# A delta-rule recurrence on one core: the small triangular solve is started one slot earlier, the scores' transposes are put ahead of k's projection

## The chip, the cores and the metric

The kernel runs on one core of one Trainium2 chip. The metric is the time of one execution on the device in microseconds (us), as the median over several executions. TensorE is called PE in the profile, VectorE DVE, ScalarE ACT, GpSimd POOL, and SyncE, which issues all DMAs of this kernel, SP.

## The reference, cut to what matters

The input is x of shape (32, 512, 256). A gated delta-rule recurrence with 8 heads of 32 runs over the 512 tokens of each batch, two steps for each token; around it stand projections, a gate, a norm, an output projection, two layer norms and a feed-forward layer with merged low-rank weights.

```python
q, k, v = silu(x @ Wq), silu(x @ Wk), silu(x @ Wv)
log_f = log_sigmoid(x @ Wf1 @ Wf2);  beta = sigmoid(x @ Wbeta) * 2
k = l2norm(k);  k_ = -beta * k
gk = interleave(log_f, 0);  a = interleave(k_ * exp(log_f), k_);  bb = interleave(k, k)
kk, vv, qq = interleave(0, k), interleave(0, v), interleave(0, q)
for t:   # 1024 steps
    bS = einsum('bhk,bhkv->bhv', bb_t, S)
    S = exp(gk_t) * S + a_t * bS + kk_t * vv_t
    o_t = einsum('bhk,bhkv->bhv', qq_t, S)
y = rmsnorm(o[1::2] * sigmoid(x @ Wog1 @ Wog2)) * norm_w
x = layernorm(x + y @ Wo)
x = layernorm(x + x @ (W.T + lora.T) + b)
```

## The kernel before

The tokens are cut into 32 groups of 512 (2 x 16 batches, 16 tokens of each). The recurrence is run in blocks of 8 tokens (16 steps): inside a block the steps' dependence on each other is a 16 x 16 unit triangular matrix, whose inverse is worked out once, so that a block costs a few small matmuls. A group has 8 chunks of such blocks, and the program is a pipeline of iterations j, one for each group, each of 8 **slots** 0 to 7. In slot n of iteration j:

- PE runs `deltas` (L732) of the chunk before, `updates` (L724), `right_sides` (L741) of chunk n, and then `dense<n>`, the part of the dense work that is hung on this slot: v's projection and the first scores in slot 0, the gate and further scores in slot 1, `dense2` and `dense3` (k's and q's projections `project` L582, the scores' transposes `turn_scores` L614, the transposes `turn_rows` L624, the beta and f matmuls L596 and L599), the feed-forward (L634) in slot 4, the sums of squares (L605) in slot 5, the output projection (L695) in slot 6, the inverse's transposes (L706) in slot 7.
- DVE runs `update` (o_col L1105, change L1113; it waits for `updates` of this slot) and `turn_right_sides` (L1121, x_now L1124; it waits for `right_sides`), and then its own share of dense work. x_now is what `deltas` of the next slot need.
- ACT runs `delta_part` (L860, which waits for DVE's `update` of the slot), `query_part` (qs L881, which waits for x_now), `mask_part` (wa_now L874), and then its share.
- POOL adds and decays the state (L475, L479) after DVE's `update`, and adds the bias to h_row (L491, four instructions) between slots 3 and 4, once eight steps of the solve are done.

The dense work belongs to neighbouring groups: iteration j makes k, q, f and beta of group j + 2, scores and the inverse of group j + 1, and the output of groups j - 1 to j - 3. Each engine runs its instructions in the order in which they are written; semaphores carry the waits.

The inverse of group j + 1 is made like this. `turn_scores` transposes the scores a_low into PSUM (stage "nt", 4 fills); ACT sets inv to the identity (L977) and copies the fills into `low` (L990, 8 copies); `solve` on DVE runs 15 steps p = 0 to 14 of a product (L1162) and a sum (L1166) each; ACT spreads inv into `both` (L1051); PE transposes that in slot 7. Before the change `solve` runs its steps 0 to 7 at the end of slot 3, 8 to 10 and, behind the clamp of dd (L1228), 11 to 14 at the end of slot 4, and ACT spreads inv at the end of slot 5.

PSUM banks: three banks are handed round in the order of a list, `FILLS`, and `claim` makes PE wait until the bank's fill three places back in the list has been drained by ACT or DVE. From k on the list reads before: k0, k1, nt0, nt1, q0, q1, ht0, ht1, beta0, f0, ff0, ff1, yss0, yss1. So the second transposes of `turn_rows`, ht1, wait until q0 has been drained, that is for ACT's Silu of q (L1001), and f0 waits until ht0 has been drained (L1005).

Of the kernel before, what the change touches and what calls it, by code (L numbers as in the profile page):

```python
# [8 lines left out]
ACT = mybir.ActivationFunctionType  # L9
# [6 lines left out]
HF = D // P  # L16
HPH = P // HD
GB = 2
# [4 lines left out]
ROWS = TB * STEPS  # L23
# [51 lines left out]
def delta_block(nc, x, xt, wq, wk, wv, wf1, wf2, wbeta, wog1, wog2, norm_w, wo, ffn_wt, ffn_b,  # L75
# [8 lines left out]
    TILES = CH * CT  # L84
# [18 lines left out]
              "q": (2, HF), "beta": (2, HF), "f": (2, HF), "yss": (-1, HF), "kss": (2, HF), "nt": (1, 4),  # L103
              "wo": (-1, TT // 2), "tt": (1, 4)}
    PER_BANK = {s: GB if s == "nt" else 1 for s in STAGES}
    FILLS = [(s, i) for some in ("v", "gate", "small", "k", "nt", "q", "ht", ("beta", "f"), "ff", "yss", "kss", "wo", "tt")
             for i in range(2) for s in ((some,) if isinstance(some, str) else some)
             if i < (1 if s in ("beta", "f") else STAGES[s][1])]
    RING = 3
# [6 lines left out]
    with ExitStack() as ctx:  # L116
# [24 lines left out]
        small = sb("small", [P, TOK])  # L141
# [3 lines left out]
        k_col = sb("k_col", [P, HF, TOK])  # L145
# [4 lines left out]
        w_col = sb("w_col", [P, TILES, HD])  # L150
        w_row = [sb(f"w_row{c}", [P, TILES, HD]) for c in range(2)]
        gate = [sb(f"gate{c}", [P, HF, TOK]) for c in range(2)]
# [3 lines left out]
        inv = sb("inv", [P, ROWS, HPH, ROWS])  # L156
        both = sb("both", [P, ROWS, HPH, GB, ROWS])
# [50 lines left out]
        def bank(stage, i):  # L208

            if i >= 2:  # L210
                return psum[3 + i - 2]
            if i == 1 and stage in ("beta", "f"):
                return psum[3 if stage == "beta" else 4]
            return psum[5 + AT[(stage, i)] % RING]
# [9 lines left out]
        filled = {s: signal(f"{s}_filled", n) for s, (_, n) in STAGES.items()}  # L224
# [16 lines left out]
        w_turned = signal("w_turned", 1)  # L241
# [4 lines left out]
        inv_set = signal("inv_set", 1)  # L246
# [39 lines left out]
        def there(g):  # L286

            return 0 <= g < G if isinstance(g, int) else True
# [236 lines left out]
        def _(pe):  # L525
# [82 lines left out]
            def turn_scores(j):  # L608
                pe.wait_ge(low_copied.handle, low_copied.at(j + 1, CH))
                for k in range(4):  # L610
                    ps = claim(j, "nt", k)
                    for i in range(4):
                        src = a_low[:, 4 * k + i, :, :].rearrange("p b m -> p (b m)")
                        mm = pe.transpose(ps[:, i * P:(i + 1) * P], src, ident)  # L614
                    mm.then_inc(filled["nt"].handle, 1)
# [40 lines left out]
                    mm.then_inc(filled["small"].handle, 1)  # L656

            def dense2(j):
                if there(j + 2):
                    for f in range(HF):  # L660
                        project(j, "k", 0, f)
                if there(j + 1):
                    turn_scores(j)

            def dense3(j):
                if there(j + 2):
# [186 lines left out]
        def _(act):  # L853
# [68 lines left out]
            def iteration(j, c):  # L922
# [53 lines left out]
                if next_one:  # L976
                    act.activation(inv[:, :, :, :], cf[:, C_EYE:C_EYE + ROWS * ROWS].rearrange(  # L977
                        "p (i j) -> p i j", i=ROWS).unsqueeze(2).to_broadcast([P, ROWS, HPH, ROWS]),
                                   ACT.Copy).then_inc(inv_set.handle, 1)
                if front:  # L980
                    for f in range(HF):
                        act.wait_ge(filled["k"].handle, filled["k"].at(j + 2, f + 1))
                        act.activation(k_col[:, f, :], bank("k", f)[:, :], ACT.Silu).then_inc(drained["k"].handle, 1)
                if next_one:
                    for k in range(4):
                        act.wait_ge(filled["nt"].handle, filled["nt"].at(j + 1, k + 1))
                        src = bank("nt", k)[:, :].rearrange("p (i h b j) -> p i h b j", i=4, h=HPH, b=GB)
                        for b in range(GB):
                            half = slice(b * TILES, (b + 1) * TILES)
                            act.activation(low[half, 4 * k:4 * k + 4, :, :], src[half, :, :, b, :], ACT.Copy,  # L990
                                           scale=-1.0).then_inc(drained["nt"].handle, 1)

                scan_part(3)
                query(3)
# [29 lines left out]
                if front:  # L1024
                    act.activation(ss_col[:, :, :], k_col[:, :, :], ACT.Square).then_inc(k_squared.handle, 1)
                    act.wait_ge(e_floored.handle, e_floored.at(j + 2, 1))
                    act.activation(dd[:, :, :, 1:SLOTS], dd[:, :, :, 1:SLOTS], ACT.Ln,
                                   bias=one).then_inc(f_logged.handle, 1)

                scan_part(5)  # L1030
                query(5)
# [8 lines left out]
                if front:  # L1040
# [3 lines left out]
                                       bias=eps_l2).then_inc(drained["kss"].handle, 1)  # L1044
                    act.wait_ge(drained["kss"].handle, drained["kss"].at(j + 2, HF))
                    act.activation(ss_col[:, :, :], ss_col[:, :, :], ACT.Exp, scale=-0.5).then_inc(r_ready.handle, 1)
                if next_one:
                    act.wait_ge(solve_step.handle, solve_step.at(j + 1, 2 * (ROWS - 1)))
                    for b in range(GB):
                        half = slice(b * TILES, (b + 1) * TILES)  # L1050
                        act.activation(both[half, :, :, b, :], inv[half, :, :, :], ACT.Copy).then_inc(inv_spread.handle, 1)  # L1051

                scan_part(6)
                query(6)
# [20 lines left out]
        def _(dve):  # L1075
# [50 lines left out]
            def mask_pair(g, c, k):  # L1126
                for i in reversed(range(PAIR)):
                    if i:
                        made = held(dve, until, a_filled.at(g, k + 1))
                        dve.wait_ge(set_up.handle, N_SET_UP)  # L1130
                        dve.wait_ge(a_filled.handle, made)
                    else:
                        made = held(dve, until, low_copied.at(g, PAIR * k + 1))
                        dve.wait_ge(set_up.handle, N_SET_UP)
                        dve.wait_ge(low_copied.handle, made)
                    src = a_banks[i][:, :, :, ROWS:RQ]
                    dve.copy_predicated(chunk(aq[c], PAIR * k + i).rearrange("p m (b t) -> p m b t", b=GB),  # L1137
                                        ci[:, :].rearrange("p (b t) -> p b t", b=GB).unsqueeze(1).to_broadcast(
                                            list(src.shape)), src).then_inc(aq_masked.handle, 1)
# [29 lines left out]
            def iteration(j, c):  # L1169
# [32 lines left out]
                turn_part(1)  # L1202
                if next_one:
                    mask_pair(j + 1, 1 - c, 2)
                    mask_pair(j + 1, 1 - c, 3)

                scan_part(2)
                turn_part(2)
                if next_one:
                    for i in range(2):  # L1210
                        some = slice(i * TILES // 2, (i + 1) * TILES // 2)
                        last = dve.transpose(w_row[1 - c][:, some, :], w_col[:, some, :])
                    last.then_inc(w_turned.handle, 1)

                scan_part(3)
                turn_part(3)
                if next_one:
                    dve.wait_ge(inv_set.handle, inv_set.at(j + 1, 1))
                    dve.wait_ge(drained["nt"].handle, drained["nt"].at(j + 1, 4 * GB))
                    solve(j + 1, 0, 8)  # L1220

                scan_part(4)
                turn_part(4)
                if next_one:
                    solve(j + 1, 8, 11)
                if front:
                    dve.wait_ge(drained["f"].handle, drained["f"].at(j + 2, HF))
                    dve.tensor_scalar(dd[:, :, :, 1:SLOTS], dd[:, :, :, 1:SLOTS], MAX_FALL, None,  # L1228
                                      ALU.min).then_inc(e_floored.handle, 1)
                if next_one:  # L1230
                    solve(j + 1, 11, ROWS - 1)

                scan_part(5)
                turn_part(5)
# [124 lines left out]
```

## Time and profile before

| | |
|---|---|
| median of 3 runs | 2539.0 us (2536.97 to 2541.99) |
| profiled execution, its own time | 2536.87 us |
| its span | 2535.0 us |
| PE busy | 2121.5 us (84%) |
| DVE busy | 1764.5 us (70%) |
| ACT busy | 1627.2 us (64%) |
| POOL busy | 838.3 us (33%) |
| the chain that ended last | PE 57%, DVE 22%, issue 15%, ACT 5%, DMA 1% |

The span is the profiled execution from its first to its last instruction; its own time has 1.87 us around that. The chain is followed back from the last instruction to what released each wait; that it passes through both PE and DVE says that in some slots PE's own work sets the pace and in others DVE's.

### The profile page before, as it was taken

The numbers are of one execution on the slowest core, as the hardware profiler recorded it, in microseconds if no ns is written. First come the engines' busy times: TensorE is split into PE (matmuls) and PEld (weight loads), VectorE is DVE, ScalarE is ACT, GpSimd is POOL, SyncE is SP. The second block draws the span as 40 slices with busy tenths as digits, with TensorE's granted clock in tenths as the row PEclk, the third lists the DMA queues.
The fourth block names the chain that finished last, engine by engine and source line by source line (L and its number), as shares of the span: only waits on it lengthen the run. The fifth ranks groups of instructions, "written<-read, shape, count | busy, mean of one in ns | idle before, by whom it ended". The sixth has DMA issues, their size and how long they took to land.

```text
span 2535.0 us, 191611 instructions
## 1 busy us (share of the span) xinstructions
PE 2121.5 (84%) x85960; PEld 1591.0 (63%) x85960; DVE 1764.5 (70%) x4196; ACT 1627.2 (64%) x3048; POOL 838.3 (33%) x805
## 2 busy tenths in 40 slices
PE   6777888888888888888888888888888888889784
PEld 3556666666666666666666666666666666666573
DVE  3567567777766777766777766677876677776643
ACT  3656566666666666666666666666667666666554
POOL 1133233333333333323333323333333333332330
PEclk8889999999999999999999999999999999999886
DMA  3343244443344444344444344444334444433431
GB/s 100 85 120 113 90 132 136 139 130 98 120 130 139 133 129 121 105 123 138 137 131 131 96 124 136 131 139 128 111 117 124 137 137 132 130 98 120 131 111 38
DMA packets 558366, 305.46 MB, mean 120 GB/s; under 512 B 417186, under 2 KB 517152, under 8 KB 558240
## 3 DMA queue, kind: packets, MB, share of 16 engines
q1 hardware_dynamic: 558240, 304.19, 40.4%
q14 instruction: 97, 0.79, 0.1%
q8 instruction: 29, 0.48, 0.1%
HBM read 35.66 MB, written 16.78 MB: 21 GB/s over the span
## 4 chain that ended last, share of the span: by engine, by line
PE 57%; DVE 22%; issue 15%; ACT 5%; DMA 1%; SPq 0%; DVEq 0%; ACTq 0%
PE bank L582 15%; PE bank L716 8%; PE bank L741 7%; PE wide L724 7%; PE wide L732 4%; DVE uq_a L1162 4%; DVE inv L1166 4%; ACT t_t L890 3%; DVE dd L1248 3%; PE bank L655 3%; PE bank L614 2%; DVE change L1113 2%; PE bank L605 2%; PE bank L599 2%; DVE k_col L1267 2%
## 5 line engine op out<-in xcount | busy, mean ns | idle before, releaser
L475 POOL TENSOR_TENSOR state<-state,change 128x512 f32<-128x512 f32 x252 | 347.2, 1378 | 1354.2 <-DVE change L1113 1354.2
L582 PE MATMUL bank<-x_col,w_kqv 128*128 128x512 f32 x768 | 372.4, 622 | 55.9 <-issue 43.7
L741 PE MATMUL bank<-uq_now,s_now 32*32 32x24 f32 x32768 | 364.4, 187 | 9.0 <-issue 7.3
L741 PEld LDWEIGHTS bank<-uq_now,s_now 32*32 32x32 f32 x32768 | 350.4, 105 | 14.4 <-issue 10.2
L724 PE MATMUL wide<-wa_now,delta 32*32 32x80 f32 x16512 | 350.2, 234 | 3.2 <-ACT wa_now L874 2.5
L860 ACT ACTIVATE delta<-wide 128x256 f32<-128x256 f32 x256 | 98.1, 383 | 388.0 <-DVE change L1113 383.6
L1137 DVE COPY_PREDICATED aq<-ci,bank 128x128 f32<-128x128 int32 x256 | 77.3, 302 | 346.7 <-PE bank L716 218.3
L724 PEld LDWEIGHTS wide<-wa_now,delta 32*32 32x32 f32 x16512 | 308.3, 108 | 4.9 <-DMA wa_now<-aq 2.8
L479 POOL TENSOR_TENSOR state<-state,edge 128x512 f32<-128x512 f32 x252 | 292.7, 1161 | 19.8
L732 PEld LDWEIGHTS wide<-x_now,t_now 32*32 32x32 f32 x16448 | 174.0, 108 | 149.0 <-issue 148.6
L1105 DVE TENSOR_TENSOR o_col<-qs,wide 128x64 f32<-128x64 f32 x512 | 89.2, 215 | 252.2 <-PE wide L724 249.9
L582 PEld LDWEIGHTS bank<-x_col,w_kqv 128*128 128x128 f32 x768 | 139.5, 195 | 197.7 <-issue 181.6
L732 PE MATMUL wide<-x_now,t_now 32*32 32x32 f32 x16448 | 200.7, 197 | 59.0 <-issue 41.5
L874 ACT ACTIVATE wa_now<-w_row,cf 128x256 f32<-128x256 f32 x512 | 229.6, 498 | 0.8
L1166 DVE TENSOR_TENSOR inv<-inv,uq_a 128x60 f32<-128x60 f32 (+7 forms) x480 | 217.0, 452 | 16.5
L1162 DVE TENSOR_TENSOR uq_a<-low,inv 128x60 f32<-128x60 f32 (+7 forms) x480 | 200.5, 418 | 17.4 <-ACT low L990 4.1
L1113 DVE STREAM_TRANSPOSE change<-wide 128x256 f32<-128x256 f32 x512 | 197.9, 424 | 1.3
L881 ACT ACTIVATE qs<-bank 128x128 f32<-128x128 f32 x256 | 70.9, 277 | 177.1 <-DVE x_now L1124 177.0
L918 ACT ACTIVATE a_low<-bank 128x256 f32<-128x256 f32 x256 | 134.0, 625 | 72.1 <-PE bank L716 71.9
L716 PEld LDWEIGHTS bank<-uq_a,w_a 32*32 32x32 f32 x8192 | 99.8, 109 | 111.1 <-issue 111.1
L491 POOL TENSOR_TENSOR h_row<-h_row,bias_row 128x256 f32<-128x256 f32 x128 | 89.0, 726 | 225.1 <-DVE inv L1166 172.9
L716 PE MATMUL bank<-uq_a,w_a 32*32 32x48 f32 x8192 | 108.7, 208 | 59.0 <-issue 58.9
(96 smaller groups left out, 3827.4 us busy)
## 6 DMA issues: line engine op xcount, KB each, us to landing
s_now<-state SPq DMA_DIRECT2D x256, 256.0 KB
uq_now<-uqv SPq DMA_DIRECT2D x256, 192.0 KB
t_now<-t_t SPq DMA_DIRECT2D x256, 128.0 KB
uq_a<-uqv SPq DMA_DIRECT2D x64, 384.0 KB, 3.1
low<-uqv SPq DMA_DIRECT2D x64, 384.0 KB
x_col<-in_xt_dram SPq DMA_DIRECT2D x32, 512.0 KB, 3.9
w_a<-w_col SPq DMA_DIRECT2D x64, 256.0 KB, 3.7
inv<-w_col SPq DMA_DIRECT2D x64, 256.0 KB
```

The lines of the kernel that those rows point to most:

```text
L475: pool.tensor_tensor(mine, mine, change[m % 2][:, :, :, :].rearrange("p m b v -> p (m b) v"), ALU.add).then_inc(s_added.handle, 1)
L479: pool.tensor_tensor(mine, mine, decay.unsqueeze(2).to_broadcast([P, CT * GB, HD]), ALU.mult).then_inc(state_ready.handle, 1)
L582: mm = pe.matmul(ps[:, :], w_kqv[:, a, w, f * P:(f + 1) * P], x_col[:, a, :], start=a == 0, stop=a == KT - 1)
L716: mm = pe.matmul(a_banks[m // CT][quarter(h), m % CT, :, :].rearrange("p b r -> p (b r)"), w_a[c][quarter(h), m, :], uq_of(uq_a[c], m % HF ...
L724: mm = pe.matmul(up_bank[quarter(h), m % HF, m // HF, :].rearrange("p (k e) -> p k e", e=PIECE), delta[quarter(h), m, :], wa_now[quarter(h ...
L732: mm = pe.matmul(p2_bank[quarter(h), m % HF, m // HF, :], t_now[quarter(h), m, :], x_now[quarter(h), m, :], start=True, stop=True)
L741: mm = pe.matmul(p1_bank[quarter(h), m, b, :], s_now[quarter(h), m, b, :], uq_of(uq_now, m % HF)[quarter(h), m // HF, b * RQ:(b + 1) * RQ] ...
L874: act.activation(dst, rows, ACT.Copy, scale=cf[:, C_TAKE + b:C_TAKE + b + 1]).then_inc(w_masked.handle, 1)
L918: act.activation(a_low[:, :, :, n * CT:(n + 1) * CT].rearrange("p i b m -> p m b i"), a_banks[i][:, :, :, 0:ROWS], ACT.Copy).then_inc(low_ ...
L1113: last = dve.transpose(dst[:, f, :, :], up_bank[:, f, :, 0:GB * HD])
L1162: dve.tensor_tensor(step, low[:, p + 1:ROWS, :, p:p + 1].to_broadcast(size), inv[:, p:p + 1, :, 0:width].to_broadcast(size), ALU.mult).the ...
L1166: dve.tensor_tensor(inv[:, p + 1:ROWS, :, 0:width], inv[:, p + 1:ROWS, :, 0:width], step, ALU.add).then_inc(solve_step.handle, 1)
```

## The change

- `FILLS`: nt now stands before k, so from there on the list reads nt0, nt1, k0, k1, q0, q1, ht0, ht1 and so on; ht1 stands three places behind q0 as before.
- PE: in slot 2 the scores' transposes run before k's projection.
- ACT: in slot 2 the 8 copies into `low` run before the two Silus of k; the two copies into `both` run at the end of slot 4 in place of slot 5.
- DVE: the two transposes of W (w_row) run in slot 1, between the third and the fourth pair of masks, in place of slot 2; `solve` runs steps 0 to 6 at the end of slot 2 and 7 to 14 at the end of slot 3; in slot 4 only the clamp of dd is left.

```diff
-    FILLS = [(s, i) for some in ("v", "gate", "small", "k", "nt", "q", "ht", ("beta", "f"), "ff", "yss", "kss", "wo", "tt")
+    FILLS = [(s, i) for some in ("v", "gate", "small", "nt", "k", "q", "ht", ("beta", "f"), "ff", "yss", "kss", "wo", "tt")
...
             def dense2(j):
-                if there(j + 2):
-                    for f in range(HF):
-                        project(j, "k", 0, f)
                 if there(j + 1):
                     turn_scores(j)
+                if there(j + 2):
+                    for f in range(HF):
+                        project(j, "k", 0, f)
...
+                if next_one:
+                    act.wait_ge(solve_step.handle, solve_step.at(j + 1, 2 * (ROWS - 1)))
+                    for b in range(GB):
+                        half = slice(b * TILES, (b + 1) * TILES)
+                        act.activation(both[half, :, :, b, :], inv[half, :, :, :], ACT.Copy).then_inc(inv_spread.handle, 1)
 
                 scan_part(5)
...
                 if next_one:
                     mask_pair(j + 1, 1 - c, 2)
-                    mask_pair(j + 1, 1 - c, 3)
-
-                scan_part(2)
-                turn_part(2)
-                if next_one:
                     for i in range(2):
                         some = slice(i * TILES // 2, (i + 1) * TILES // 2)
                         last = dve.transpose(w_row[1 - c][:, some, :], w_col[:, some, :])
                     last.then_inc(w_turned.handle, 1)
+                    mask_pair(j + 1, 1 - c, 3)
+
+                scan_part(2)
+                turn_part(2)
+                if next_one:
+                    dve.wait_ge(inv_set.handle, inv_set.at(j + 1, 1))
+                    dve.wait_ge(drained["nt"].handle, drained["nt"].at(j + 1, 4 * GB))
+                    solve(j + 1, 0, 7)
 
                 scan_part(3)
                 turn_part(3)
                 if next_one:
-                    dve.wait_ge(inv_set.handle, inv_set.at(j + 1, 1))
-                    dve.wait_ge(drained["nt"].handle, drained["nt"].at(j + 1, 4 * GB))
-                    solve(j + 1, 0, 8)
+                    solve(j + 1, 7, ROWS - 1)
 
                 scan_part(4)
                 turn_part(4)
-                if next_one:
-                    solve(j + 1, 8, 11)
                 if front:
                     dve.wait_ge(drained["f"].handle, drained["f"].at(j + 2, HF))
                     dve.tensor_scalar(dd[:, :, :, 1:SLOTS], dd[:, :, :, 1:SLOTS], MAX_FALL, None,
                                       ALU.min).then_inc(e_floored.handle, 1)
-                if next_one:
-                    solve(j + 1, 11, ROWS - 1)
```

The rows on PE in the loop over the groups, slots 2 and 3, with the number of each PSUM bank and the semaphores that are waited for (L582 in slot 2 is k's projection and in slot 3 q's; rows with L620 belong to ht1, those with L599 to f). Before the change:

```order
L582 MATMUL bank5<-x_col,w_kqv 128x512 [waits gate_drained]
L582 MATMUL bank3<-x_col,w_kqv 128x512 [waits gate_drained]
L614 MATMUL bank4<-cf,a_low 128x128 [waits small_drained]
L614 MATMUL bank5<-cf,a_low 128x128 [waits k_drained]
L582 MATMUL bank3<-x_col,w_kqv 128x512 [waits k_drained]
L620 REGISTER_ALU [waits q_drained]
L624 MATMUL bank3<-cf,h_row 128x128 [waits h0_normed]
```

And after it:

```order
L614 MATMUL bank5<-cf,a_low 128x128 [waits gate_drained]
L614 MATMUL bank3<-cf,a_low 128x128 [waits gate_drained]
L582 MATMUL bank4<-x_col,w_kqv 128x512 [waits small_drained]
L582 MATMUL bank5<-x_col,w_kqv 128x512 [waits nt_drained]
L582 MATMUL bank3<-x_col,w_kqv 128x512 [waits nt_drained]
L620 REGISTER_ALU [waits q_drained]
L624 MATMUL bank3<-cf,h_row 128x128 [waits h0_normed]
L599 MATMUL bank5<-small,w_second 128x512 [waits ht_drained]
```

The transposes L614 have moved ahead of the first two L582 (k); the second k now waits for the first drain of nt, and the waits of slot 3 on q_drained and ht_drained are where they were.

The rows on DVE around the end of the solve's part in slot 2. In the changed program step 6 of the solve ends ahead of slot 3's `update` (L1105, L1113), and step 7 stands behind its x_now:

```order
L1166 TENSOR_TENSOR inv<-inv,uq_a 128x36x7
L1105 TENSOR_TENSOR o_col<-qs1,wide 128x4x2x8 x2
L1113 STREAM_TRANSPOSE change1<-wide 128x4x64 x2
L1121 TENSOR_TENSOR bank0<-bank0,uqv1 128x16x8
L1124 STREAM_TRANSPOSE x_now<-bank0 128x256
L1162 TENSOR_TENSOR uq_a<-low,inv 128x256
```

In the program before, the same five rows of slot 3 stood behind the transposes of W:

```order
L1212 STREAM_TRANSPOSE w_row0<-w_col 128x1024 x2
L1105 TENSOR_TENSOR o_col<-qs1,wide 128x4x2x8 x2
L1113 STREAM_TRANSPOSE change1<-wide 128x4x64 x2
L1121 TENSOR_TENSOR bank0<-bank0,uqv1 128x16x8
L1124 STREAM_TRANSPOSE x_now<-bank0 128x256
L1162 TENSOR_TENSOR uq_a<-low,inv 128x60
```

What was step 0 behind slot 3's x_now is now step 7, and seven steps have moved from behind `update` to ahead of it.

## Rows read from the trace of the kernel before

**Rows 1.** Timeline of PE: start, length (us), line, tiles, count [idle before <-releaser].

```profile
1209.77 0.75 PE L732 MATMUL wide<-x_now,t_now 32*32 32x32 f32 x64
...
1222.81 1.53 PE L706 MATMUL bank<-cf,both 128*128 128x128 f32 x12 [0.73 <-DVE x_row L1287]
...
1231.89 1.56 PE L716 MATMUL bank<-uq_a,w_a 32*32 32x48 f32 x128 [1.80 <-issue]
...
1252.13 3.70 PE L582 MATMUL bank<-x_col,w_kqv 128*128 128x512 f32 x8 [0.55 <-issue]
...
1257.50 0.75 PE L732 MATMUL wide<-x_now,t_now 32*32 32x32 f32 x64
...
1264.88 1.04 PE L624 MATMUL bank<-cf,h_row 128*128 128x128 f32 x8
...
1266.21 0.69 PE L599 MATMUL bank<-small,w_second 32*128 32x512 f32 x1
...
1268.12 0.75 PE L732 MATMUL wide<-x_now,t_now 32*32 32x32 f32 x64
...
1275.60 0.75 PE L732 MATMUL wide<-x_now,t_now 32*32 32x32 f32 x64
...
1281.57 1.13 PE L605 MATMUL bank<-r_col,cf 128*128 128x512 f32 x2 [0.98 <-DVE h_row L1239]
...
1284.34 0.75 PE L732 MATMUL wide<-x_now,t_now 32*32 32x32 f32 x64
```

**Rows 2.** Timeline of DVE, slots 1 to 5 of the same iteration.

```profile
1247.89 0.30 DVE L1137 COPY_PREDICATED aq<-ci,bank 128x128 f32<-128x128 int32 x1 [2.64 <-PE bank L716]
...
1252.34 2.33 DVE L1212 STREAM_TRANSPOSE w_row<-w_col 128x1024 f32<-128x1024 f32 x2
1259.48 0.35 DVE L1105 TENSOR_TENSOR o_col<-qs,wide 128x64 f32<-128x64 f32 x2 [4.81 <-PE wide L724]
...
1263.15 0.27 DVE L1162 TENSOR_TENSOR uq_a<-low,inv 128x112 f32<-128x112 f32 x1
...
1267.91 0.43 DVE L1162 TENSOR_TENSOR uq_a<-low,inv 128x256 f32<-128x256 f32 x1
...
1271.35 0.30 DVE L1121 TENSOR_TENSOR bank<-bank,uqv 128x128 f32<-128x128 f32 x1 [0.21 <-PE bank L741]
...
1272.06 1.20 DVE L1162 TENSOR_TENSOR uq_a<-low,inv 128x252 f32<-128x252 f32 x1
...
1278.80 0.22 DVE L1162 TENSOR_TENSOR uq_a<-low,inv 128x60 f32<-128x60 f32 x1
...
1279.22 0.35 DVE L1105 TENSOR_TENSOR o_col<-qs,wide 128x64 f32<-128x64 f32 x2
...
1280.86 1.25 DVE L1239 TENSOR_TENSOR h_row<-h_row,bank 128x512 f32<-128x512 f32 x2
```

**Rows 3.** Timeline of ACT, slots 2, 3 and 5 of the same iteration.

```profile
1253.42 1.07 ACT L977 ACTIVATE inv<-cf 128x1024 f32<-128x1024 f32 x1
...
1256.36 3.18 ACT L990 ACTIVATE low<-bank 64x256 f32<-64x256 f32 x8
...
1262.51 1.04 ACT L997 ACTIVATE r_col<-y_col 128x1024 f32<-128x1024 f32 x1
1263.45 0.58 ACT L1001 ACTIVATE q_col<-bank 128x512 f32<-128x512 f32 x1
...
1265.57 1.08 ACT L1005 ACTIVATE a_low<-bank 128x512 f32<-128x512 f32 x2
...
1281.94 1.48 ACT L1035 ACTIVATE r_col<-bank,cf 128x512 f32<-128x512 f32 x2
```

**Rows 4.** Timeline of POOL around the end of slot 3.

```profile
1268.97 2.78 POOL L491 TENSOR_TENSOR h_row<-h_row,bias_row 128x256 f32<-128x256 f32 x4 [5.98 <-DVE inv L1166]
1271.70 1.28 POOL L475 TENSOR_TENSOR state<-state,change 128x512 f32<-128x512 f32 x1
```

**Rows 5.** Windows, end of another iteration's slot 5: engines' busy time, granted clock, DMA.

```profile
1133.00:1136.60 3.60, 3.60 (x9) 1.05 (x9) 3.57 (x5) 2.55 (x4) 0.27 (x1) 0.58 0.00 0
```

More of the change, by code:

```diff
@@ L658, in dense2 @@
             def dense2(j):
+                if there(j + 1):
+                    turn_scores(j)
                 if there(j + 2):
@@ L661, in dense2 @@
                         project(j, "k", 0, f)
-                if there(j + 1):
-                    turn_scores(j)
             def dense3(j):
@@ L979, in iteration @@
                                    ACT.Copy).then_inc(inv_set.handle, 1)
-                if front:
-                    for f in range(HF):
-                        act.wait_ge(filled["k"].handle, filled["k"].at(j + 2, f + 1))
-                        act.activation(k_col[:, f, :], bank("k", f)[:, :], ACT.Silu).then_inc(drained["k"].handle, 1)
                 if next_one:
@@ L991, in iteration @@
                                            scale=-1.0).then_inc(drained["nt"].handle, 1)
+                if front:
+                    for f in range(HF):
+                        act.wait_ge(filled["k"].handle, filled["k"].at(j + 2, f + 1))
+                        act.activation(k_col[:, f, :], bank("k", f)[:, :], ACT.Silu).then_inc(drained["k"].handle, 1)
                 scan_part(3)
@@ L1046, in iteration @@
                     act.activation(ss_col[:, :, :], ss_col[:, :, :], ACT.Exp, scale=-0.5).then_inc(r_ready.handle, 1)
-                if next_one:
[L1048 to L1051, printed above, removed]
                 scan_part(6)
@@ L1204, in iteration @@
                     mask_pair(j + 1, 1 - c, 2)
+                    for i in range(2):
+                        some = slice(i * TILES // 2, (i + 1) * TILES // 2)
+                        last = dve.transpose(w_row[1 - c][:, some, :], w_col[:, some, :])
+                    last.then_inc(w_turned.handle, 1)
                     mask_pair(j + 1, 1 - c, 3)
@@ L1209, in iteration @@
                 if next_one:
[L1210 to L1213, printed above, removed]
+                    dve.wait_ge(inv_set.handle, inv_set.at(j + 1, 1))
+                    dve.wait_ge(drained["nt"].handle, drained["nt"].at(j + 1, 4 * GB))
+                    solve(j + 1, 0, 7)
                 scan_part(3)
```

## The prediction

> **What bounds the kernel now.** The table of the front matter gives the chain as PE and DVE in turns, so I did not read the shares of the whole span but one iteration of the loop, engine by engine. The first view is the timeline of PE. An iteration runs from `deltas` at 1209.77 to the same instruction at 1284.34, 74.57 us [rows 1]. Slot 3 begins at 1257.50, slot 4 at 1268.12, slot 5 at 1275.60 and slot 6 at 1284.34 [rows 1]. The reader should look at the idle time before each row. In slots 2 to 4 there is none but some 0.6 us of branching ahead of the dense part, so there PE's own work sets the pace. In slot 5 the second sum of squares waits 0.98 us for DVE's h_row; in slot 7 the transposes wait 0.73 us for DVE's x_row; in slot 0 the scores stand idle for 1.80 us [rows 1], because their operands are staged by a DMA that waits for the last DVE product of group j + 2. So from slot 5 to slot 0 DVE sets the pace.
>
> The second view is the timeline of DVE. It shows why. In slot 2 DVE is idle for 4.81 us and in slot 1 for 2.64 us, but in slot 4 it works off the rest of the solve until the moment at which slot 5's `update` starts, 1279.22, and that start has no idle time before it [rows 2]. From there to the end of slot 7 DVE runs without a gap. Its train starts with h_row at 1280.86 [rows 2]; the iteration is as long as PE takes from the release in slot 0 to h_row, plus that train. What counts for the change is therefore one number: how much earlier or later h_row starts.
>
> **What there is to gain.** With no solve in slot 4, h_row would start when PE lets it. In slot 4 L1121, released by PE's `right_sides`, started 1271.35 - 1268.12 = 3.23 us after the slot, and the next work 0.71 us behind it [rows 1, 2]. For slot 5 that is 1275.60 + 3.23 + 0.71 = 1279.54, against 1280.86 now: 1.32 us earlier. The 0.98 us of PE in slot 5 goes too. So the change can give some 1.0 to 1.3 us an iteration, and only if slot 5 begins no later than it does now.
>
> **What is free.** The transposes of W take 2.33 us and now stand in front of a mask that had 2.64 us of idle time before it [rows 2]; they fit, and if they did not, at most the difference would fall on scores that PE fills late in slot 1. The swap on PE costs nothing: the same instructions run, and the new wait of the second k for the drain of nt0 falls due after transposes and first k, by when ACT is through with it (below). The copies into `both` move from behind slot 5's work to a stretch of slot 4 in which ACT waited for DVE; they must be done by slot 7.
>
> **What it costs: slot 3's update is late.** This is the term that decides.
>
> (1) The transposes start at 1252.13, where k's projection did [rows 1]. ACT is not ready: it sets inv from 1253.42 for 1.07 us, and copies into `low` for 3.18 us [rows 3]. The copies end at about 1254.4 + 3.18 = 1257.6; before that `solve` can't start. DVE has been idle since x_now, about 1252.4.
>
> (2) Steps 1 to 6 took 1267.91 - 1263.15 = 4.76 us. Step 0 is as small as step 14, which took 1279.22 - 1278.80 = 0.42 us, plus the pipeline overlap, say 0.5 [rows 2]. No POOL work falls here. DVE is free at 1257.6 + 5.26 = 1262.85. Slot 3's `update` was released by PE at 1259.48 [rows 2]; it is late by 3.4 us. DVE alone could bear that: x_now would be made at some 1264.5, and PE's next `deltas` stand at 1268.12.
>
> (3) But ACT waits behind it. `delta_part` of slot 3 waits for `update`, and ACT is in order, so everything ACT does in slot 3 is queued behind it. In slot 5, where ACT followed `update` without other waits, its first dense work came 1281.94 - 1279.22 = 2.72 us after it [rows 2, 3]. The Square then takes 0.94 us up to the Silu of q0, and this 0.58 us [rows 3]. So q0 is drained at 1262.85 + 2.72 + 0.94 + 0.58 = 1267.1.
>
> (4) PE waits for that. ht0 is done at 1264.88 + 0.52 = 1265.4 [rows 1], and ht1 needs q0's bank. It runs from 1267.1 to 1267.65 and not to 1265.92: +1.7 us. f0 needs the drain of ht0. ACT comes to it after the second Silu, at about 1267.65, and one of the two copies takes 0.54 us [rows 3]; f0 starts at 1268.2 and not at 1266.21 [rows 1]: +2.0 us. Slot 4 begins at 1270.1 and slot 5 at 1277.6, 2.0 us later than now.
>
> (5) h_row then starts at 1277.6 + 3.23 + 0.71 = 1281.54, against 1280.86: +0.68 us. PE itself is 2.0 - 0.98 = 1.0 us late at slot 6, which is less than it waits for DVE in slots 6 to 0. So the iteration takes 0.68 us more.
>
> **The second half of the solve.** Steps 7 to 14 now run in slot 3 beside POOL's state work and, since step 7 comes at once, beside the four bias adds. An L1162 that takes 0.42 us alone took 1.20 us from 1272.06, while POOL's L475 ran from 1271.70 to 1272.98 [rows 2, 4]: each waited for the other's end. Undisturbed, the eight steps take about 6 us, the state work adds 1 us, and the bias adds something between nothing and their own 2.78 us [rows 4]; I take 2. They end at 1264.5 + 9 = 1273.5, or 1271.7 to 1274.5 by the bounds. Slot 4's `update` is released at 1270.1 + 1.98 = 1272.1 (1.98 is 1259.48 - 1257.50 [rows 1, 2]), so it is up to 2.4 us late; x_now follows 1.7 us behind, by 1276.2 at the latest, ahead of slot 5 at 1277.6. I cost it at nothing; its cover is thin, 1.4 us at the far bound. The Trainium skill, in "SBUF — State Buffer", section on who interferes with whom, has it that a DVE instruction with two SBUF inputs and a GpSimd instruction exclude each other for their whole length; by that rule the far bound, 2.78 us, holds rather than my 2, and the cover is the thin one. No bias add stands beside a solve in this trace.
>
> **The sum.** 28 of the 32 iterations have all parts (the first two have no turn_rows, the last two no q and no k). 28 x 0.68 = 19 us. On the profiled execution's own 2536.87 that is 2556; the median of the runs is 2.1 us above it, which makes 2558. I add 2 us for the clock (below) and forecast 2560 us, +0.8%. Differences under 0.2%, 5 us, are taken as none.
>
> **Rivals.**
>
> *The stall stays small and the gain comes (faster).* For: the solve leaves slot 4, where it is plainly in the way, and gain and loss differ by one small sum. Against: the loss is a chain of five measured lengths. The point that decides is how late slot 5 starts: 1.32 us or less instead of 2.0. That needs the low copies or the first seven steps to be 0.7 us shorter than in (1) and (2), or q0's drain to come early. With no stall at all the iteration is 1.0 to 1.3 us shorter: 2539 - 28 x 1.15 = 2507; with half of it about 2530. Chance 0.22.
>
> *Loss and gain cancel (no change).* Slot 5 is 1.2 to 1.5 us late. 2534 to 2544. Chance 0.08.
>
> *The clock falls in slot 3 (slower by more).* At the end of a slot 5 in which PE had stood idle twice, the granted clock was 0.58 for 3.60 us [rows 5], between the two levels of 1.2 and 2.4 GHz; at full clock the same work would take 3.6 x 0.58 = 2.1 us, so the fall cost 1.5 us. Not every iteration shows it. The new stall of 1.7 us lies between transposes and small matmuls in the stretch that is critical, so there a fall is paid in full, up to 28 x 1.5 = 42 us more; while slot 5 loses one of its idle times, which is worth nothing, since DVE is late there anyway. The Trainium skill, "TensorE: Matmul & The Clock Gate", section on why this matters, says that idle between bursts of matmuls takes the clock back to its half rate; by that rule each iteration might pay, the sum would be 2600, and it has a chance of its own in what follows. The slot 3 of before shows no fall. Chance 0.22 that a third or more of the iterations pay: 2570 to 2600.
>
> *The forecast as it stands*, only the stall and few falls: 2545 to 2570. Chance 0.48.
>
> **Numbers.** Slower by over 0.2%: 0.48 + 0.22 = 0.70. Same 0.08. Faster 0.22. The range leaves out the better half of the faster case (0.12) and the last of the clock's (0.05): 2524 to 2594. The likeliest case's own range is 2545 to 2570.
>
> **What would show it.** In the profile after: the copies into `low` end near 5.3 us after k's old start and DVE stands idle up to them, about 5 us in slot 2 (1); slot 3's `update` starts with no idle time, 3.4 us behind PE's release (2); ACT waits some 5 us for DVE's change in slot 3 (3); the transposes L624 are split, the second half with 1.7 us of idle time released by ACT's q_col, and slot 3 takes 12.6 in place of 10.62 us (4); slot 5 shrinks from 8.74 to 7.8 us (5). The forecast is wrong if L624 isn't split, if the granted clock is low in slots 3 and 4, or if x_now of slot 4 comes after PE's `deltas` of slot 5.

## The result, and the profile after

The changed kernel is slower: 2622.47 us in the median of 4 runs (2618.89 to 2629.29) against 2538.34, a ratio of 1.0332, 95% interval 1.0306 to 1.0359. The direction was forecast; the size was not: 84 us where 22 were expected, and 2622 lies outside the range of 2524 to 2594.

From the page of the changed kernel, the span, the engines' busy time and the engines' shares of the chain:

```profile
span 2617.6 us, 191583 instructions
PE 2175.2 (83%) x85960; PEld 1634.7 (62%) x85960; DVE 1772.5 (68%) x4196; ACT 1621.4 (62%) x3048; POOL 869.7 (33%) x805
...
PE 46%; DVE 26%; issue 15%; ACT 13%; DMA 0%; DVEq 0%; SPq 0%; ACTq 0%
```

PE is busy for 54 us more than before with the same number of instructions, and ACT, which had 5% of the chain, has 13%. Where that happens is seen in the timeline of PE, slots 2 to 5 of one iteration (the stretch that [rows 1] shows for before):

```profile
1212.47 1.96 PE L614 MATMUL bank<-cf,a_low 128*128 128x128 f32 x16 [0.65 <-issue]
...
1217.80 0.75 PE L732 MATMUL wide<-x_now,t_now 32*32 32x32 f32 x64
...
1225.16 0.60 PE L624 MATMUL bank<-cf,h_row 128*128 128x128 f32 x4
1227.47 0.65 PE L624 MATMUL bank<-cf,h_row 128*128 128x128 f32 x4 [1.70 <-ACT q_col L1001]
...
1230.69 1.06 PE L599 MATMUL bank<-small,w_second 32*128 32x512 f32 x1
1231.68 1.08 PE L732 MATMUL wide<-x_now,t_now 32*32 32x32 f32 x64
1232.55 2.34 PE L724 MATMUL wide<-wa_now,delta 32*32 32x80 f32 x64
...
1240.58 0.75 PE L732 MATMUL wide<-x_now,t_now 32*32 32x32 f32 x64
...
1244.43 1.98 PE L605 MATMUL bank<-r_col,cf 128*128 128x512 f32 x4 [0.68 <-issue]
```

The transposes L624 are split, and the second half waits 1.70 us for ACT's drain of q, as forecast. The wait of the second sum of squares in slot 5 is gone. What was not in the forecast's main case stands behind the stall: a matmul of f (L599) takes 1.06 us and `updates` (L724) 2.34 us. In the kernel before, at the same place, they took 0.59 and 1.31 us:

```profile
1267.61 0.59 PE L599 MATMUL bank<-small,w_second 32*128 32x512 f32 x1
...
1268.73 1.31 PE L724 MATMUL wide<-wa_now,delta 32*32 32x80 f32 x64
```

The windows of this stretch in the changed kernel, with PE's granted clock in the third column from the end, say why:

```profile
1223.00:1225.20 2.20, 2.20 (x7) 0.93 (x6) 2.17 (x8) 0.75 (x3) 0.99 (x1) 1.00 0.32 121
1225.20:1227.50 2.30, 0.60 (x6) 0.36 (x4) 2.20 (x4) 2.30 (x5) 1.77 (x3) 1.00 0.00 0
1227.50:1229.50 2.00, 2.00 (x9) 1.59 (x11) 1.93 (x3) 1.35 (x4) 2.00 (x3) 0.83 0.00 0
1229.50:1231.70 2.20, 2.20 (x9) 0.40 (x6) 2.06 (x5) 1.09 (x2) 1.05 (x2) 0.50 0.00 0
1231.70:1234.70 3.00, 3.00 (x133) 3.00 (x136) 1.94 (x7) 2.42 (x4) 0.00 (x0) 0.50 0.13 44
```

In the second window PE is busy for 0.60 of 2.30 us; in the windows after it the granted clock falls to 0.50, that is from 2.4 to 1.2 GHz, and it stays there into slot 4. In the next iteration slot 4 ran at 0.58 in the mean and took 10.85 us (first two lines below). One of the 27 iterations has the stall, 1.66 us, and no fall (last two lines):

```profile
1295.49:1308.47 12.98, 10.65 (x281) 6.56 (x280) 12.25 (x27) 6.55 (x13) 5.80 (x6) 0.96 0.16 51
1308.47:1319.32 10.85, 10.35 (x273) 9.02 (x272) 5.10 (x16) 7.87 (x12) 2.76 (x2) 0.58 0.19 60
...
2235.57:2248.00 12.43, 10.09 (x281) 6.58 (x280) 11.73 (x27) 6.24 (x13) 5.53 (x6) 1.00 0.16 53
2248.00:2255.48 7.48, 6.83 (x274) 6.00 (x273) 6.12 (x17) 5.35 (x10) 2.92 (x3) 1.00 0.27 88
```

That iteration took 74.75 us in all, no more than the 74.94 of before. Slots 3 and 4 of the kernel before, for comparison:

```profile
1257.50:1268.12 10.62, 9.94 (x281) 6.48 (x280) 7.93 (x21) 7.23 (x17) 2.31 (x2) 1.00 0.19 62
1268.12:1275.60 7.48, 6.82 (x273) 5.99 (x272) 5.76 (x13) 5.11 (x9) 5.11 (x6) 1.00 0.27 88
```

The mean length of each slot, read off the timeline of PE from one `deltas` to the next over 27 iterations of each kernel, in us:

| | slot 3 | slot 4 | slot 5 | slot 6 | slot 7 | slot 0 | slot 1 | slot 2 | iteration | slot 4 over 8 us |
|---|---|---|---|---|---|---|---|---|---|---|
| before | 10.63 | 7.48 | 9.22 | 7.58 | 6.98 | 13.17 | 10.75 | 9.13 | 74.94 | 0 of 27 |
| changed | 13.39 | 9.22 | 7.48 | 7.59 | 6.77 | 13.55 | 10.73 | 9.23 | 77.94 | 26 of 27 |

The iteration is 3.0 us longer; times 28 that is 84 us, the whole difference. Slots 3 and 4 lose 4.5 us, slot 5 gives back 1.7.

### The profile page after: what moved, and what is told of

Its sections match the earlier page's. It is cut to its first block, busy times and chain, and to the rows that moved or that the text cites. A ratio compares the mean times of both kernels' runs of the same rounds, so it can differ in the third digit from the quotient of the medians.

```text
span 2617.6 us, 191583 instructions
## 1 busy us (share of the span) xinstructions
PE 2175.2 (83%) x85960; PEld 1634.7 (62%) x85960; DVE 1772.5 (68%) x4196; ACT 1621.4 (62%) x3048; POOL 869.7 (33%) x805
## 4 chain that ended last, share of the span: by engine, by line
PE 46%; DVE 26%; issue 15%; ACT 13%; DMA 0%; DVEq 0%; SPq 0%; ACTq 0%
PE bank L716 8%; PE wide L724 7%; PE bank L741 7%; PE bank L582 6%; PE bank L634 5%; PE wide L732 4%; DVE dd L1245 3%; DVE uq_a L1162 3%; ACT t_t L890 3%; ACT low L986 3%; DVE inv L1166 3%; PE bank L655 3%; DVE change L1113 3%; DVE w_col L1275 2%; DVE x_now L1124 2%
## 5 line engine op out<-in xcount | busy, mean ns | idle before, releaser
L582 PE MATMUL bank<-x_col,w_kqv 128*128 128x512 f32 x768 | 371.2, 620 | 36.6 <-issue 24.1
L741 PE MATMUL bank<-uq_now,s_now 32*32 32x24 f32 x32768 | 372.5, 190 | 8.3 <-issue 8.3
L724 PE MATMUL wide<-wa_now,delta 32*32 32x80 f32 x16512 | 375.4, 244 | 3.6 <-ACT wa_now L874 2.5
L741 PEld LDWEIGHTS bank<-uq_now,s_now 32*32 32x32 f32 x32768 | 360.9, 108 | 12.7 <-issue 9.3
L724 PEld LDWEIGHTS wide<-wa_now,delta 32*32 32x32 f32 x16512 | 331.1, 114 | 6.5 <-DMA wa_now<-aq 2.8
L1162 DVE TENSOR_TENSOR uq_a<-low,inv 128x60 f32<-128x60 f32 (+7 forms) x480 | 210.5, 438 | 179.9 <-ACT low L986 165.6
L479 POOL TENSOR_TENSOR state<-state,edge 128x512 f32<-128x512 f32 x252 | 303.9, 1206 | 19.8
L732 PEld LDWEIGHTS wide<-x_now,t_now 32*32 32x32 f32 x16448 | 180.4, 110 | 191.1 <-issue 190.6
L732 PE MATMUL wide<-x_now,t_now 32*32 32x32 f32 x16448 | 207.2, 199 | 68.9 <-issue 40.7
L582 PEld LDWEIGHTS bank<-x_col,w_kqv 128*128 128x128 f32 x768 | 140.2, 196 | 177.7 <-issue 152.9
L1105 DVE TENSOR_TENSOR o_col<-qs,wide 128x64 f32<-128x64 f32 x512 | 88.9, 215 | 230.3 <-PE wide L724 226.2
L1113 DVE STREAM_TRANSPOSE change<-wide 128x256 f32<-128x256 f32 x512 | 197.8, 424 | 1.3
L634 PE MATMUL bank<-w_ffn,a_low 128*128 128x256 f32 x512 | 131.5, 414 | 19.4 <-issue 18.0
```

Source lines behind the costliest of these rows:

```text
L479: pool.tensor_tensor(mine, mine, decay.unsqueeze(2).to_broadcast([P, CT * GB, HD]), ALU.mult).then_inc(state_ready.handle, 1)
L582: mm = pe.matmul(ps[:, :], w_kqv[:, a, w, f * P:(f + 1) * P], x_col[:, a, :], start=a == 0, stop=a == KT - 1)
L634: mm = pe.matmul(ps[:, t * D:(t + 1) * D], h_col[:, a, own], w_ffn[:, a, :], start=a == 0, stop=a == KT - 1)
L724: mm = pe.matmul(up_bank[quarter(h), m % HF, m // HF, :].rearrange("p (k e) -> p k e", e=PIECE), delta[quarter(h), m, :], wa_now[quarter(h ...
L732: mm = pe.matmul(p2_bank[quarter(h), m % HF, m // HF, :], t_now[quarter(h), m, :], x_now[quarter(h), m, :], start=True, stop=True)
L741: mm = pe.matmul(p1_bank[quarter(h), m, b, :], s_now[quarter(h), m, b, :], uq_of(uq_now, m % HF)[quarter(h), m // HF, b * RQ:(b + 1) * RQ] ...
```

## The experiments

All were timed beside the kernel before on the same chip; ratios are to that kernel. The theory after the result: the stall is there as forecast and costs little, and the fall of the clock behind it costs the rest, in nearly every iteration.

**Only the orders.** The solve is put back to its old places, and the copies into `both` too. What is left is the order in slot 2, the list of banks and W's place.

```diff
-                    solve(j + 1, 0, 7)
...
-                    solve(j + 1, 7, ROWS - 1)
+                    solve(j + 1, 0, 8)
...
+                    solve(j + 1, 8, 11)
...
+                    solve(j + 1, 11, ROWS - 1)
```

> The changed kernel with the solve at its old places (steps 0 to 7 in slot 3, 8 to 14 in slot 4 around the clamp) and the copies into both back in slot 5; what stays of the change is the order in slot 2 (transposes before k, on PE and ACT, with the list of banks) and W's transposes in slot 1. Theory (stall and clock: the loss comes from the first seven steps of the solve ahead of slot 3's update): these orders are free, 2538 us, within 5. Rival (the new order in slot 2 or W's transposes cost something of their own): 2550 or more, with slot 1 or 2 longer than 10.7 and 9.2 us.

Measured: 2540.05 us, ratio 1.0013 (0.9999 to 1.0028), iteration 75.02 us. These parts are free; the loss comes with the solve's new places and the copies into `both`, which moved along with it.

**The stall filled.** The same changed kernel, with PE kept at work in it.

```diff
             def turn_rows(j):
                 for i in range(TT // 2):
+                    if i == 1 and there(j + 2):
+                        pe.wait_ge(drained["nt"].handle, drained["nt"].at(j + 1, 4 * GB))
+                        for a in range(KT):
+                            pe.matmul(psum[3][:, :], w_kqv[:, a, 1, 0:P], x_col[:, a, :],
+                                      start=a == 0, stop=a == KT - 1)
                     ps = claim(j, "ht", i)
```

> The changed kernel with two useless full matmuls (128x512, some 1.85 us together) on PE ahead of the wait for the drain of q0, into a bank that is free there and is overwritten later; nothing that is used is changed. PE has work where it stood idle for 1.7 us. Theory (of the loss in slots 3 and 4 about 2 us is the stall and the rest the fall of the granted clock that the idle time brings): the clock stays at full in slots 3 and 4, slot 3 takes 12.6 to 12.9 us, slot 4 again 7.5, and the time is what the prediction gave for the stall alone, 2555 to 2570. Rival (slot 4 is long because DVE comes late out of the solve that POOL's bias adds slow down, or for another reason on PE): slot 4 stays at 8.9 or more and the time at 2620.

Measured: 2548.28 us, ratio 1.0044 (1.0029 to 1.0060). The timeline of PE, where L622 is the filler, and the windows of slots 3 and 4 of that iteration:

```profile
1196.85 0.60 PE L629 MATMUL bank<-cf,h_row 128*128 128x128 f32 x4
1197.29 1.88 PE L622 MATMUL bank<-x_col,w_kqv 128*128 128x512 f32 x4
1199.15 0.65 PE L629 MATMUL bank<-cf,h_row 128*128 128x128 f32 x4
...
1201.96 0.75 PE L737 MATMUL wide<-x_now,t_now 32*32 32x32 f32 x64
```

```profile
1189.48:1201.96 12.48, 11.80 (x286) 7.22 (x285) 11.74 (x27) 6.27 (x14) 5.54 (x6) 1.00 0.17 53
1201.96:1209.44 7.48, 6.83 (x274) 5.99 (x273) 6.13 (x17) 5.34 (x10) 2.93 (x3) 1.00 0.27 88
```

ht1 starts as late as in the changed kernel, 2.3 us after ht0, and slot 3 takes 12.48 us. But the clock is 1.00 and slot 4 takes 7.48 us; it is 7.45 to 7.52 us in all 27 iterations. 74 of the 84 us are gone by adding 1.9 us of useless work to each iteration. So the fall of the clock is shown to be nearly the whole loss, and the rival, that slot 4 is long because DVE is late, is out. The one iteration of the changed kernel without a fall says the same with nothing added. The time is below the 2555 to 2570 of this expectation, and within the 2545 to 2570 that the forecast gave for the stall with few falls: an iteration takes 75.13 us, 0.19 over before and not 0.68.

**q drained early.** ACT's two Silus of q stand ahead of `delta_part` of slot 3.

```diff
+                if front:
+                    for f in range(HF):
+                        act.wait_ge(filled["q"].handle, filled["q"].at(j + 2, f + 1))
+                        act.activation(q_col[:, f, :], bank("q", f)[:, :], ACT.Silu).then_inc(drained["q"].handle, 1)
                 scan_part(3)
                 query(3)
```

> The changed kernel with ACT's two Silus of q put ahead of its share of slot 3's recurrence (delta_part), so that the drain of q0 no longer waits for DVE's late update. Theory (the stall comes through ACT's order): the idle time of 1.7 us before ht1 goes, the one of f0 for the drain of ht0 stays below 1 us, the granted clock stays near full, slot 3 takes 11.0 to 11.7 us, and with slot 5 shorter by 1.3 the time is 2505 to 2540. Rival (the late update of slot 3 costs by itself, through x_now, the state or POOL): slot 3 stays over 12 us and the time over 2580.

Measured: 2634.52 us, ratio 1.0379 (1.0356 to 1.0402). This missed. The timeline of PE and ACT in slot 3:

```profile
1232.60 1.04 PE L624 MATMUL bank<-cf,h_row 128*128 128x128 f32 x8
1233.57 1.12 PE L596 MATMUL bank<-small,w_second 8*128 8x512 f32 x2
1236.12 0.69 PE L599 MATMUL bank<-small,w_second 32*128 32x512 f32 x1 [1.43 <-ACT a_low L1005]
...
1238.69 1.08 PE L732 MATMUL wide<-x_now,t_now 32*32 32x32 f32 x64
```

```profile
1234.52 1.06 ACT L1001 ACTIVATE r_col<-y_col 128x1024 f32<-128x1024 f32 x1
1235.46 1.09 ACT L1005 ACTIVATE a_low<-bank 128x512 f32<-128x512 f32 x2
```

The stall only moved. ht0 and ht1 now run together, but f0 waits for the drain of ht0, which still stands behind ACT's recurrence and the Square, and that wait of 1.43 us brings the clock down as well: in this iteration the granted clock of slot 4 is 0.59, and slot 4 is over 8 us in 26 of 27. I had priced the wait at under 1 us, because I forgot the Square.

**All four drained early.** As the one before, with the drains of ht0 and ht1 moved along. The solve is cut as in the changed kernel.

```diff
+                if out_of:
+                    for i in range(TT // 2):
+                        act.wait_ge(filled["ht"].handle, filled["ht"].at(j - 2, i + 1))
+                        act.activation(h_col[:, :, 2 * i * P:2 * (i + 1) * P],
+                                       bank("ht", i)[:, :].rearrange("p (a t) -> p a t", a=KT),
+                                       ACT.Copy).then_inc(drained["ht"].handle, 1)
                 scan_part(3)
```

> The changed kernel with ACT's drains of q0, q1, ht0 and ht1 all ahead of its share of slot 3's recurrence; the solve stays cut 7 and 8, so DVE's update of slot 3 is as late as in the changed kernel. The run before this one moved only q's Silus, and the stall went from ht1 to f0. Theory (the late update costs only through ACT's order, and the rest is the clock): PE has no idle time in slot 3 but the branch, slot 3 takes 10.6 to 10.9 us, slot 4 7.5, the granted clock is full there, and the time falls to where the cut into 3, 7 and 5 steps is: 2495 to 2510. Rival (the late update costs by itself): slot 3 or 4 stay longer by 1 us or more, 2530 or more.

Measured: 2526.34 us, ratio 0.9971 (0.9957 to 0.9985). Slots 3 and 4 are as the theory has them, 10.63 and 7.53 us in the mean, at full clock:

```profile
1175.37:1185.98 10.61, 9.93 (x282) 6.47 (x281) 9.93 (x25) 4.76 (x12) 3.67 (x4) 1.00 0.19 63
1185.98:1193.55 7.57, 6.88 (x274) 6.01 (x274) 7.16 (x19) 4.85 (x9) 3.21 (x4) 1.00 0.27 87
```

DVE's update of slot 3 is as late as in the changed kernel, 5.30 us after the slot began, and it costs slot 3 nothing once ACT no longer carries it to PE. So the path of the stall is shown: DVE's solve, ACT's delta, ACT's drains, PE's banks. The time is 16 us above the expectation's upper end and under the rival's 2530. Most of that is in slot 0, 14.25 us in the mean, over 14.5 in 16 of 27 iterations; these iterations take 75.06 us, the other 11 take 73.45. In one of the long ones the clock in slot 0 was 0.89:

```profile
1140.77:1155.61 14.84, 11.90 (x520) 7.87 (x521) 10.18 (x32) 11.86 (x23) 5.73 (x8) 0.89 0.68 176
```

Why slot 0 is caught so much more often here than in the other kernels (before: 4 of 27) no run tells. Slot 5, 7.86 us here, is 0.38 longer than in the cut into 3, 7 and 5 steps below; that was not tried apart.

**The kernel before with a late ACT.** Nothing of the change; two more table loads on ACT.

```diff
+                act.preload_act_table_set("natural_log_exp_and_others")
+                act.preload_act_table(ACT.Silu)
                 if front:
                     for f in range(HF):
                         act.wait_ge(filled["q"].handle, filled["q"].at(j + 2, f + 1))
```

> The kernel before, with nothing of the change; ACT only loads its activation table twice more (1.28 us each by the profile) ahead of q's Silu in slot 3, so that q0 is drained some 2.6 us later. By the rows of before ht1 would wait about 1.2 us and f0 start 1.6 us later. Theory (idle time of PE at this place brings the clock down, whatever its cause): the granted clock falls in slots 3 and 4 of most iterations, slot 3 takes 12.2 us or more and slot 4 8.5 or more, 2590 to 2640. Rival (the fall needs what is particular to the changed kernel, the transposes ahead of k or the solve beside POOL): slot 3 takes 12.2, slot 4 7.5, about 2583.

Measured: 2622.92 us, ratio 1.0357 (1.0334 to 1.0379). The timeline of PE:

```profile
1219.58 0.65 PE L624 MATMUL bank<-cf,h_row 128*128 128x128 f32 x4 [1.41 <-ACT q_col L1003]
...
1222.67 1.06 PE L599 MATMUL bank<-small,w_second 32*128 32x512 f32 x1
1223.66 1.08 PE L732 MATMUL wide<-x_now,t_now 32*32 32x32 f32 x64
1224.54 2.34 PE L724 MATMUL wide<-wa_now,delta 32*32 32x80 f32 x64
```

A stall of 1.4 us of another cause brings the same fall: the granted clock is 0.50 from 1221.6 to 1226.7 here, and slot 4 is over 8 us in 17 of 27 iterations. In the others slots 3 and 4 take 12.18 and 7.48 us. So neither the transposes ahead of k nor the solve beside POOL is needed for it. That the time is the changed kernel's own is chance: the iterations without a fall take 76.13 us here, 1.2 more than before, because the solve still stands in slot 4 and slot 5 gives little back, and the falls bring the mean to 77.33. The length of the idle time does not alone decide how often it is caught: 1.41 us was caught in 17 of 27, but 1.43 us with q drained early in 26 of 27, as the 1.64 to 1.72 us of the changed kernel.

**Three, seven and five steps.** The stall is avoided where it begins: only as many steps stand ahead of slot 3's update as end by its release; the last five stand in slot 4 behind the clamp, and the copies into `both` in slot 5 again.

```diff
-                    solve(j + 1, 0, 7)
+                    solve(j + 1, 0, 3)
...
-                    solve(j + 1, 7, ROWS - 1)
+                    solve(j + 1, 3, 10)
...
+                    solve(j + 1, 10, ROWS - 1)
```

> The changed kernel with the solve cut otherwise: steps 0 to 2 in slot 2, 3 to 9 in slot 3, 10 to 14 in slot 4 behind the clamp; the copies into both back in slot 5. Three steps end about 1.9 us after the copies into low, when PE releases slot 3's update. Theory: no stall in slot 3 (10.6 us), slot 4 7.5, slot 5 7.5 to 7.8, and the gain of 1.0 to 1.3 us an iteration that the prediction named as what is to be had: 2500 to 2512. Rival (the end of the solve in slot 4 still holds DVE, or the train of DVE from h_row on is not what sets slots 5 to 0): 2530 to 2545.

Measured: 2497.75 us, ratio 0.9842 (0.9816 to 0.9868), faster than both kernels and 2 us under the range expected. The timeline of DVE at the start of slots 3 and 5, and the windows of slots 3, 4 and 5:

```profile
1159.21 0.26 DVE L1162 TENSOR_TENSOR uq_a<-low,inv 128x60 f32<-128x60 f32 x1 [5.20 <-ACT low L986]
...
1161.14 0.35 DVE L1105 TENSOR_TENSOR o_col<-qs,wide 128x64 f32<-128x64 f32 x2
...
1178.67 0.22 DVE L1166 TENSOR_TENSOR inv<-inv,uq_a 128x60 f32<-128x60 f32 x1
1179.21 0.35 DVE L1105 TENSOR_TENSOR o_col<-qs,wide 128x64 f32<-128x64 f32 x2 [0.31 <-PE wide L724]
...
1181.14 1.25 DVE L1238 TENSOR_TENSOR h_row<-h_row,bank 128x512 f32<-128x512 f32 x2
```

```profile
1159.17:1169.78 10.61, 9.93 (x281) 6.47 (x280) 9.71 (x24) 6.42 (x14) 3.50 (x4) 1.00 0.19 63
1169.78:1177.23 7.45, 6.81 (x273) 6.02 (x272) 6.74 (x14) 6.14 (x10) 4.90 (x5) 1.00 0.27 88
1177.23:1184.70 7.47, 6.77 (x265) 4.48 (x265) 6.77 (x18) 3.63 (x7) 2.32 (x2) 1.00 0.27 88
```

Slot 3's update starts 1161.14 - 1159.17 = 1.97 us after the slot, on time; slot 5's update now waits 0.31 us for PE, where before DVE was the late one, and slot 5 takes 7.47 us. An iteration takes 73.56 us, 1.38 less than before.

**Four, six and five steps.** The edit is shown against the version before this one.

```diff
-                    solve(j + 1, 0, 3)
+                    solve(j + 1, 0, 4)
-                    solve(j + 1, 3, 10)
+                    solve(j + 1, 4, 10)
```

> As the cut into 3, 7 and 5 steps, but 4, 6 and 5: slot 3's update is then 0.8 us late, and q0 is drained as much later, which the old order covered (it was drained 1.4 us before ht1 came to it). Both theories: no stall, within 5 us of the run with 3, 7 and 5, about 2498. If it is slower by 10 us or more, the cover is thinner than the rows said.

Measured: 2497.53 us, ratio 0.9853 (0.9833 to 0.9873), the same. The cover of q0's drain holds for a fourth step; between four steps and seven it is used up.

**A filler in slot 0.** In the version with 3, 7 and 5 steps.

```diff
             def dense0(j):
                 if there(j + 1):
                     project(j, "v", 2, 0)
+                if there(j) and there(j + 1):
+                    pe.wait_ge(drained["tt"].handle, drained["tt"].at(j, 4))
+                    for a in range(KT):
+                        pe.matmul(psum[3][:, :], w_kqv[:, a, 2, 0:P], x_col[:, a, :],
+                                  start=a == 0, stop=a == KT - 1)
```

> The cut into 3, 7 and 5 steps with two useless full matmuls on PE in slot 0, behind v's first projection, where PE stands idle 1.8 us before the first scores; their result is overwritten and used by nothing. In that kernel slot 0 takes 14.7 us in 8 of some 28 iterations with the clock low, and else 13.3 or 12.5. Theory (the same clock loss, in slot 0): no slot 0 over 13.6, 2483 to 2492. Rival (the two matmuls delay the scores, or slot 0 is long for the DMA's sake): 2497 or more.

Measured: 2499.82 us, ratio 0.9866 (0.9844 to 0.9889); against 0.9842 without the filler that is no gain. Both theories had a part: slot 0 is nowhere over 13.4 us (7 of 27 were over 14.5), but iterations whose slot 7 was long and whose slot 0 was then short, 12.3 to 12.7 us, now have 13.0 to 13.4 there. In the two traces the full iterations do get shorter, 73.35 us in place of 73.56, 6 us over 27 of them; but the first transposes of `turn_rows`, with which the start of the pipeline ends, stand at 301.15 us and not at 286.89. So in the iterations the filler takes back a part of what the clock gives, and the start takes the rest; what lengthened the start was not tried.

## Why the prediction was wrong

Right, and shown on the chip:

- (1) and (2): DVE is idle for 5.20 us up to the end of the copies into `low`, and its update starts 1223.09 - 1217.80 = 5.29 us after slot 3 began (the row of L1105 below) in place of 1.98, so 3.3 us late; 3.4 was forecast.
- (3) and (4): the stall sits where it was put, with 1.70 us, and at full clock it makes slot 3 12.46 us (the stall filled, where a filler of 1.88 us stands in its place) or 12.43 us (the one iteration without a fall) where 12.6 was forecast. That the late update reaches slot 3 only through ACT's order is shown by the version with all four drains early.
- The second half of the solve: 9 us were forecast. It runs from 1224.73 to the end of step 14, 1233.85, which is 9.1. POOL's four adds took 3.44 us beside it, and a product of 240 elements 0.81 where it takes 0.41 alone. Four of DVE's instructions were lengthened like this, by some 0.4 us each, 1.6 us in all, so the far bound of 2.78 us, which the prediction had by the Trainium skill, "SBUF — State Buffer", section on who interferes with whom, was not reached. Costing the second half at nothing was right: slot 4 is 7.49 us with the stall filled. (The bounds for its end come out of the prediction's own numbers as 1271.5 and 1274.3, not 1271.7 and 1274.5; nothing hangs on it.)

```profile
1222.76 0.42 DVE L1166 TENSOR_TENSOR inv<-inv,uq_a 128x252 f32<-128x252 f32 x1
1223.09 0.34 DVE L1105 TENSOR_TENSOR o_col<-qs,wide 128x64 f32<-128x64 f32 x2
...
1224.73 1.03 DVE L1162 TENSOR_TENSOR uq_a<-low,inv 128x256 f32<-128x256 f32 x1
...
1228.31 0.81 DVE L1162 TENSOR_TENSOR uq_a<-low,inv 128x240 f32<-128x240 f32 x1
...
1233.63 0.22 DVE L1166 TENSOR_TENSOR inv<-inv,uq_a 128x60 f32<-128x60 f32 x1
```

Wrong, and the cause of the miss: the step on the clock. The forecast took "2 us for the clock" into the sum and gave 0.22 to the case that a third or more of the iterations pay 1.5 us each. 26 of 27 pay, and they pay more: 77.94 - 75.13 = 2.81 us an iteration, the difference between the changed kernel and the one with the stall filled, 76 us between the two profiled executions and 74 between the medians. The one iteration without a fall is 3.2 us under the changed kernel's mean. The size was off because the price was read at another place. [rows 5] gives a fall at the end of slot 5, behind which DVE is late anyway, and the window was 3.6 us long there; in slots 3 and 4 the fall lies over `updates` and the start of `right_sides`, or over the whole of slot 4 with the feed-forward (10.85 us), which are PE's own pace. The chance was off because I leaned on "the slot 3 of before shows no fall": it has no stall there either. The Trainium skill, "TensorE: Matmul & The Clock Gate", section on why this matters, names idle between bursts of matmuls as what takes the clock back to its half rate. The direction agrees with the traces here, but the page speaks of longer idle times than these 1.41 to 1.72 us, so that each iteration might pay did not follow from it; the runs alone show it. The 2600 that the prediction gave for that case was 22 us short, because a fall cost 2.81 x 27 / 26 = 2.9 us and not 1.5.

Wrong by a size: (5) gave 0.68 us an iteration for the stall alone, and it is 0.19. The stall made slot 3 1.84 us longer and not 2.0, and slots 5 to 0 together take 35.22 us with the stall filled in place of 36.95, 1.73 less and not 1.32. The falls of the clock in slot 5 of before (over 10 us in 8 of 27 iterations) do not explain this: these 8 iterations took 74.80 us in the mean and the other 19 took 74.99, since slot 7 was shorter in them; those falls cost nothing, as the prediction said of slot 5. What did change is that DVE's four scans took 3.26 us before and 2.97 now, and that slot 0 was over 14.5 us in 4 iterations before and in 1 now. What part each accounts for was not tried apart.

"What there is to gain", 1.0 to 1.3 us an iteration without a stall, was sound: 1.38 with the cut into 3, 7 and 5 steps.

## What to carry to other kernels

Price an idle time of PE on its critical stretch by the work behind it, not by its own length: here 1.7 us of idle cost 1.6 us an iteration as a wait (75.13 with the stall filled against 73.56 in the cut without a stall; it looks like 0.2 beside the kernel before only because the change gave back 1.4), and 2.8 us more as a clock. When work is moved ahead of a step that others wait for, follow it through each in-order engine up to the PSUM banks, and move just as much as ends before that step is released: three steps in place of seven, with the last five left in slot 4, turned a loss of 3.3% into a gain of 1.6%. To tell a stall from the clock it brings, fill it with useless matmuls and time again.

## What the runs showed of the hardware that was not expected

- An idle time of PE of 1.41 us (the kernel before with a late ACT), 1.43 us (q drained early) or 1.64 to 1.72 us (the changed kernel) among the transposes and the matmuls of 8 and 32 rows was followed by a slot 4 of over 8 us in 17, 26 and 26 of 27 iterations; where windows were laid over such a fall, the granted clock was 0.50 in the changed kernel and in the one with a late ACT. In the kernel before, without the idle time, slot 4 kept its 7.5 us in all 27.
- In the version with all drains early slot 0 was over 14.5 us in 16 of 27 iterations, before in 4, though slot 0's own instructions were the same. What decides in which iterations a given idle time brings the clock down stays open.
